# A gated delta-rule layer on one core: strict triangles built from PSUM, correction matrices kept in three buffers, and a new order of VectorE's work in each pass

## What is computed

```python
q, k, v = silu(causal_conv4(x @ w_qkv))             # 4 taps in time, per channel
g, beta = -exp(A_log) * softplus(a + dt_bias), sigmoid(b)
q, k = l2norm(q) * DK ** -0.5, l2norm(k)
def step(state, inp):
    state = state * exp(g_t)
    delta = (v_t - einsum('kv,k->v', state, k_t)) * b_t
    state = state + einsum('k,v->kv', k_t, delta)
    return state, einsum('kv,k->v', state, q_t)
y = rms_norm(out * silu(z)) @ w_out
```

## Time and profile before

| | before |
|---|---|
| median of 3 runs | 3218.49 us (3217.93 to 3222.51) |
| the profiled execution's own time | 3209.48 us |
| its span, first to last instruction | 3207.7 us |
| TensorE busy | 2926.0 us, 91% |
| VectorE busy | 2951.7 us, 92% |
| GpSimd busy | 2218.9 us, 69% |
| ScalarE busy | 1798.5 us, 56% |
| mean granted TensorE clock | 0.975 of full speed |
| chain that ended last, by engine | VectorE 62%, TensorE 22%, ScalarE 8%, issue 5% |

### The profile page before, as it was taken

How to read it: one execution, slowest core, us unless ns; L and a number is a source line. 1 busy time by engine, 2 the same in 40 slices (tenths; PEclk the granted TensorE clock), 3 DMA queues, 4 the chain that set the end, 5 groups by cost and what they waited for, 6 DMA issues and landing times.

```text
span 3207.7 us, 56507 instructions
## 1 busy us (share of the span) xinstructions
PE 2926.0 (91%) x18444; PEld 2394.4 (75%) x18444; DVE 2951.7 (92%) x9293; ACT 1798.5 (56%) x4175; POOL 2218.9 (69%) x2394
## 2 busy tenths in 40 slices
PE   7942899999999999999999999999999999999997
PEld 4421678787878877878778877788787787877876
DVE  4997899999999999999999999999999999999996
ACT  3321555565556655565555655566555665656554
POOL 0003677877777777777777777787777777777764
PEclk9975999999999999999999999999999999999999
DMA  2002555555555555555555555555555565555653
GB/s 64 1 1 66 151 142 144 143 149 156 140 146 138 156 151 140 143 141 156 144 146 135 151 157 142 144 138 155 151 145 139 142 159 146 149 134 146 159 143 85
DMA packets 541829, 427.99 MB, mean 133 GB/s; under 512 B 247009, under 2 KB 450785, under 8 KB 541537
## 3 DMA queue, kind: packets, MB, share of 16 engines
q1 hardware_dynamic: 476000, 222.98, 25.6%
q0 software_dynamic: 65536, 201.39, 24.0%
HBM read 345.61 MB, written 45.09 MB: 122 GB/s over the span
## 4 chain that ended last, share of the span: by engine, by line
DVE 62%; PE 22%; ACT 8%; issue 5%; DMA 1%; POOL 1%; POOLq 1%; DVEq 0%; SPq 0%; ACTq 0%
DVE mix L1222 12%; DVE qkv L1181 9%; PE ps L584 4%; DVE E L1169 4%; DVE rows L1201 4%; PE ps L522 3%; DVE xg L1148 3%; PE ps L526 3%; PE ps L556 3%; PE ps L569 3%; PE ps L576 3%; DVE xr L1238 3%; ACT L824 2%; ACT L841 2%; DVE outer L1234 2%
## 5 line engine op out<-in xcount | busy, mean ns | idle before, releaser
L958 POOL DMA_INDIRECT rows<-table,idx_all x1024 | 1200.1, 1172 | 382.7 <-issue 280.3
L813 ACT ACTIVATE qkv<-qkv 128x512 f32<-128x512 f32 x256 | 161.4, 630 | 603.8 <-DVE qkv L1181 603.8
L942 POOL TENSOR_SCALAR xg<-xg,rms 128x128 f32<-128x128 f32 x520 | 407.3, 798 | 7.0
L576 PE MATMUL ps<-XT,E 128*128 128x128 f32 x3072 | 400.5, 277 | 0.0
L556 PEld LDWEIGHTS ps<-X,AT 128*128 128x128 f32 x3072 | 363.4, 192 | 35.7 <-DMA X<-whole 17.9
L1222 DVE SCALAR_TENSOR_TENSOR mix<-rows,zc,mix 128x256 f32<-128x256 f32 x896 | 381.3, 491 | 0.4 <-ACT zc L824 0.4
L556 PE MATMUL ps<-X,AT 128*128 128x128 f32 x3072 | 375.2, 275 | 3.3 <-DMA X<-whole 3.3
L576 PEld LDWEIGHTS ps<-XT,E 128*128 128x128 f32 x3072 | 368.7, 192 | 0.0
L946 POOL COPY gn<-gates 128x8 f32<-128x8 f32 x64 | 12.3, 193 | 481.3 <-SPq L330 262.2
L950 POOL TENSOR_SCALAR gm<-cst,gn 128x128 f32<-128x128 f32 x512 | 340.3, 680 | 6.5
L808 ACT ACTIVATE raw<-ps 128x512 f32<-128x512 f32 x256 | 152.9, 597 | 313.5 <-PE ps L522 313.5
(11 more groups left out here) (165 smaller groups left out, 6172.5 us busy)
## 6 DMA issues: line engine op xcount, KB each, us to landing
Wvz<-wvz SPq DMA_DIRECT2D x64, 512.0 KB, 3.2
xb<-xnT SPq DMA_DIRECT2D x64, 512.0 KB, 4.5
whole<-AT SPq DMA_DIRECT2D x128, 256.0 KB
X<-whole SPq DMA_DIRECT2D x128, 256.0 KB, 4.2
XT<-whole SPq DMA_DIRECT2D x128, 256.0 KB, 4.7
wo<-woh SPq DMA_DIRECT2D x65, 256.0 KB, 4.4
Wkq<-wkq SPq DMA_DIRECT2D x64, 256.0 KB, 2.9
rows<-table,idx_all POOLq DMA_INDIRECT x1024
```

Of the source, the lines that this page charges most:

```text
L576: done = mm(ps[:, 4 + g, (a % 4) * P:(a % 4 + 1) * P], E[:, a, :], src[:, a, :], start=True, stop=True)
L942: pool.tensor_scalar(xg[:, a, :], xg[:, a, :], rms[:, a:a + 1], None, ALU.mult).then_inc(sm["y_p"], 1)
L958: pool.indirect_dma_start(rows[:, m, :], None, table[:, :], bass.IndirectOffsetOnAxis(ap=idx_all[:, f // 4, c:c + 1], axis=0)).then_inc(ga ...
```

## The change

- `triangle` multiplies straight out of PSUM bank 6, by the negated scales `nscol` (new), eight instructions that each count up `at_v`. The masked copy `km` and the added identity are gone: elements outside the strict triangle and the sign are dealt with further on (the elimination adds instead of subtracting; the off-diagonal blocks are taken as they are).
- `E` becomes three buffers `Es`, one per level, which GpSimd fills with identities once, ahead of the first step. At level 0 VectorE writes only the off-diagonal blocks (`copy_predicated`), at level 1 ScalarE copies them (`second_level`, four copies of 32 partitions), at level 2 VectorE copies one 64x64 block per task. The level matrices leave the constants.
- Since bank 6 is held until the triangles are read, `projection(1)` goes to bank 7 and `squares(0)` to bank 3.
- On VectorE the three taps of k stand inside the first half of the expert sums, after four of its eight instructions, and `half_v` comes behind the other four. The corrections of `RV` stand ahead of the taps of v. `scaled_y(0)` stands ahead of the elimination.
- The copy `xb` of the normalized input, and its transfer of 512 KB per step, are gone: `projection(4)` and `(5)` read `xnT`. `Y` now lies in `X`.

`output_weights`, which computes MT on VectorE, is the same before and after.

```diff
-C_ID, C_LE, C_GT, C_SU, C_EYE, C_MS = 0, 1, 2, 3, 4, 6
-NC = C_MS + len(LEVELS)
+C_ID, C_LE, C_GT, C_EYE, C_OFF = 0, 1, 2, 3, 5
+NC = 6
...
+    off = (p // (2 * BL) == j // (2 * BL)) & (p // BL == j // BL + 1)
...
-        E = sb("E", [P, TASKS, P])
-        Y = E
+        Es = [sb(f"E{lv}", [P, TASKS, P]) for lv in range(len(LEVELS))]
+        Y = X
...
-                sp.dma_start(xb[:, :, :], xnT[:, :, bass.ds((f // HEADS) * N, N)]).then_inc(sm["xb_in"], 16)
...
-                    sp.wait_ge(sm["at_v"], at("at_v", g + 1))
+                    sp.wait_ge(sm["at_v"], at("at_v", 4 * g + 4))
...
-                    bank = (7, 6, 7, 6, 7, 6)[u]
+                    bank = (7, 7, 7, 6, 7, 6)[u]
...
-                    pe.wait_ge(sm["e_v"], at("e_v", 2 * lv + g + 1))
+                    if lv == 1:
+                        pe.wait_ge(sm["e_s"], at("e_s", 2 * g + 2))
+                    else:
+                        pe.wait_ge(sm["e_v"], at("e_v", lv + g + 1))
...
                     products(0, 6)
-                    pe.wait_ge(sm["tap_s"], at("tap_s", 2))
-                    squares(0, 7)
-                    pe.wait_ge(sm["km_v"], at("km_v", 1))
+                    if back:
+                        pe.wait_ge(sm["x_s"], at("x_s", 2))
+                    squares(0, 3)
                     projection(1)
+                if front:
+                    pe.wait_ge(sm["ssk_v"], at("ssk_v", 1))
...
-                    pe.wait_ge(sm["ssk_v"], at("ssk_v", 1))
+                    pe.wait_ge(sm["tap_s"], at("tap_s", 4))
                     products(1, 7)
-                    pe.wait_ge(sm["tap_s"], at("tap_s", 4))
+                    pe.wait_ge(sm["at_v"], at("at_v", 8))
                     squares(1, 6)
...
+                def second_level(g):
+                    act.wait_ge(sm["e_t"], at("e_t", 3 + g))
+                    for p0, c0 in ((32, 0), (96, 64)):
+                        A(Es[1][p0:p0 + 32, 4 * g:4 * g + 4, c0:c0 + 32],
+                          ps[p0:p0 + 32, g, :].rearrange("p (a i) -> p a i", a=4)[:, :, c0:c0 + 32], ACT.Copy).then_inc(sm["e_s"], 1)
...
                     take_XT(0, 1)
+                    second_level(0)
+                    second_level(1)
...
+            for buf in Es:
+                pool.tensor_copy(buf[:, :, :], mask(C_ID, TASKS)).then_inc(zeroed, 1)
...
                     dve.wait_ge(sm["e_t"], at("e_t", 2 * lv + g + 1))
-                    V.tensor_tensor(E[:, 4 * g:4 * g + 4, :], ps[:, g, :].rearrange("p (a i) -> p a i", a=4), mask(C_MS + lv, 4), ALU.mult)\
-                        .then_inc(sm["e_v"], 1)
+                    e, new = Es[lv][:, 4 * g:4 * g + 4, :], ps[:, g, :].rearrange("p (a i) -> p a i", a=4)
+                    if lv == 0:
+                        done = V.copy_predicated(e, mask(C_OFF, 4).bitcast(U32), new)
+                    else:
+                        done = V.tensor_copy(e[64:128, :, 0:64], new[64:128, :, 0:64])
+                    done.then_inc(sm["e_v"], 1)
...
                     for a in range(4 * g, 4 * g + 4):
-                        st.did(V.scalar_tensor_tensor(out=AT[:, a, :], in0=km[:, a // R, :], scalar=scol[:, a:a + 1], in1=DT[:, a, :],
-                                                      op0=ALU.mult, op1=ALU.mult))
-                    st.wait()
-                    V.tensor_tensor(AT[:, 4 * g:4 * g + 4, :], AT[:, 4 * g:4 * g + 4, :], mask(C_ID, 4), ALU.add).then_inc(sm["at_v"], 1)
+                        V.scalar_tensor_tensor(out=AT[:, a, :], in0=ps[:, 6, (a // R) * P:(a // R + 1) * P], scalar=nscol[:, a:a + 1], in1=DT[:, a, :],
+                                               op0=ALU.mult, op1=ALU.mult).then_inc(sm["at_v"], 1)
...
-                    V.tensor_tensor(km[:, :, :], ps[:, 6, :].rearrange("p (t i) -> p t i", t=4), mask(C_SU, 4), ALU.mult).then_inc(sm["km_v"], 1)
...
-                    expert_mix(0)
+                    expert_mix(0, 2)
+                if front:
+                    for d in (1, 2, 3):
+                        tap(0, d)
+                if back:
+                    expert_mix(2, 4)
                     st.wait()
                     dve.sem_inc(sm["half_v"], 1)
-                if front:
-                    for d in (1, 2, 3):
-                        tap(0, d)
-                if back:
                     second_gated(nx)
-                    level(1, 0)
-                    level(1, 1)
...
+                if back:
+                    scaled_y(0, 1, "y0_t", "ys0_v")
...
-                    eliminate(0, 4)
-                if back:
-                    scaled_y(0, 1, "y0_t", "ys0_v")
-                if front:
-                    eliminate(4, HB - 1)
+                    eliminate(0, HB - 1)
```

More of the change, by code:

```diff
@@ L66, in constants @@
     p, j = i[:, None], i[None, :]
-    def level(n):
-        off = (p // (2 * n) == j // (2 * n)) & (p // n == j // n + 1)
-        return np.eye(P) - off
+    off = (p // (2 * BL) == j // (2 * BL)) & (p // BL == j // BL + 1)
     eye = np.broadcast_to(np.eye(BL).reshape(1, BL * BL), (P, BL * BL))
-    m = [np.eye(P), p <= j, p > j, p < j, eye[:, :P], eye[:, P:]] + [level(n) for n in LEVELS]
+    m = [np.eye(P), p <= j, p > j, eye[:, :P], eye[:, P:], off]
     m = np.stack([np.asarray(a, np.float32) for a in m], 1).reshape(P, NC * P)
@@ L525, in projection @@
                             for k in range(KD):
-                                done = mm(ps[:, bank, (t % 2) * 256:(t % 2) * 256 + 256], xb[:, k, t * P:(t + 1) * P],
+                                done = mm(ps[:, bank, (t % 2) * 256:(t % 2) * 256 + 256], xnT[:, k, pn * N + t * P:pn * N + (t + 1) * P],
                                           Wvz[:, k, 2 * P:4 * P], start=k == 0, stop=k == KD - 1)
@@ L805, in take @@
                         act.wait_ge(sm["conv_v"], last("conv_v", u + 3))
-                    bank = (7, 6, 7, 6)[u]
+                    bank = (7, 7, 7, 6)[u]
                     w = cwkq[:, u, 3:4] if u < 2 else cwv[:, u - 2, 3:4]
@@ L1205, in expert_dots, with expert_mix @@
                                     half_of(prob_all[:, n // 4, (n % 4) * 16:(n % 4) * 16 + 16], hf), ALU.mult).then_inc(sm["dot_v"], 1)
-                def expert_mix(hf):
-                    dve.wait_ge(sm["silu_e"], at("silu_e", hf + 1))
-                    for k in range(hf * (K // 2), (hf + 1) * (K // 2)):
+                def expert_mix(k0, k1):
+                    dve.wait_ge(sm["silu_e"], at("silu_e", k0 // 4 + 1))
+                    for k in range(k0, k1):
                         for s in range(2):
@@ L1237, in eliminate @@
                         v = x[:, :, j + 1:HB, 0:m]
-                        last_row[0] = st.did(V.tensor_tensor(v, v, o, ALU.subtract))
+                        last_row[0] = st.did(V.tensor_tensor(v, v, o, ALU.add))
                 def lower_products():
@@ L1319, in one_pass @@
                     level(0, 1)
-                    expert_mix(0)
-                    st.wait()
-                    dve.sem_inc(sm["half_v"], 1)
+                    expert_mix(0, 2)
                 if front:
@@ L1326, in one_pass @@
                 if back:
+                    expert_mix(2, 4)
+                    st.wait()
+                    dve.sem_inc(sm["half_v"], 1)
                     second_gated(nx)
-                    level(1, 0)
-                    level(1, 1)
                     if place["u"]:
```

38 lines of the change are left out of this document (18 added, 20 removed).

## The result

The changed kernel is slower: 3293.15 us in the median of 4 runs (3284.49 to 3296.89) against 3218.21 us (4 runs, 3212.65 to 3222.51) of the kernel before, ratio 1.023, 95% interval 1.0204 to 1.0256. The profiled execution took 3296.89 us.

The account below looks back on a forecast made before the run. It took a loop through GpSimd's gathers and scales as the bound, with VectorE's load equally long. Terms of +0.8 us a step gave +50 us, other effects −2, so 3218.5 + 48 = 3266 us, range 3200 to 3310.

Parts of the forecast that it names:

- What bounds the kernel: One step: a loop through GpSimd's gathers and scales to TensorE's transposes and tail closes it; VectorE's load closes another, equally long.
- GpSimd's loop: Differences, experts' first half, `half_v`, eight gathers, square root, eight scales, transposes, TensorE's tail, next differences: 44.53 us a step.
- VectorE's load: Masks, `km` and identity adds go: about 3.8 us of 44.53 leave VectorE; level 0's `copy_predicated` taken as 0.67 us.
- the rival of twice a mask: Level 0's `copy_predicated` costs double a mask, delaying mix, k's taps and `half_v`: +43 us more, 3309 us; chance 10%.
- Release: `half_v`, which lets GpSimd's gathers start, comes at D+11.35 instead of D+8.42 behind k's taps: +2.9 us a step.
- Gathers: GpSimd's eight gathers are held less by VectorE's two-SBUF-input instructions: −1.0 us a step, bounds 0 and −1.9.
- Scales: GpSimd's eight scales: VectorE's second mix still falls onto them, MT no longer: −0.3 us a step, bounds 0 and −1.5.
- Tail: From GpSimd's last scale to the next differences: 15.1 us instead of 15.87, VectorE now waiting for `ks_t`: −0.8 us.
- The sum: Per step, +2.9 − 1.0 − 0.3 − 0.8 = +0.8 us; over sixty-two steps +50 us.
- GpSimd is freed enough: First gather to last scale falls by more than 2.1 us, so the kernel gets faster: 3132 us, halfway 3175; 17%.
- The gathers don't matter: GpSimd's timing is a coincidence; TensorE alone is left with its holes filled: −2.7 a step, 3050 us; 5%.
- ScalarE is not late: z is emptied in time for the second difference matmul, so the step grows only +0.2: 3230 us; chance 10%.

Follow-up runs that it names:

- the first four experiments: Changed kernel with k's taps behind the release, 0.9906; corrections behind v's taps, 0.994; both orders undone, 0.9985; eight unused matmuls in TensorE's wait, 1.0073; against the kernel before.

## Why the prediction was right

The forecast was 3266 us, the result 3293, inside the range of 3200 to 3310 and on the forecast side. By its steps:

- *What bounds the kernel.* Right: GpSimd's loop became the bound, TensorE stood before the transposes (2.1 us a step in the timeline, 161 us of waiting in all, against "some 2 us, over 100").
- *VectorE's load.* 2.9 us a step left it, not 3.8. What was removed came to about 3.8; other instructions grew, such as the first two outer products of the elimination, which now stand beside GpSimd's scales and took 0.29 and 0.35 us in the step from 1541.71 on, where they had taken 0.16 and 0.17. This didn't matter, as assumed. `copy_predicated`, the copies of level 1 on ScalarE and those of level 2, groups of instructions (xcount | busy us, mean ns | idle before):

```profile
L1179 DVE COPY_PREDICATED E<-cst,ps 128x512 f32<-128x512 uint32 x128 | 93.7, 733 | 14.4 <-PE ps L550 13.3
...
L823 ACT ACTIVATE E<-ps 32x128 f32<-32x128 f32 x256 | 69.0, 269 | 6.8 <-PE ps L550 0.6
L1181 DVE COPY E<-ps 64x256 f32<-64x256 f32 x128 | 54.7, 428 | 91.0 <-PE ps L550 91.0
```

  0.73 us where I took 0.67, so the rival of twice a mask falls; 0.43 for a 64x256 copy, against 0.33 taken.
- *Release.* +2.73 against +2.9. The second difference matmul does wait for ScalarE's z, and `level_E(0)` begins at D+2.20 instead of D+1.72: 0.48 late, taken as 0.6. Its row before, where D was 1500.34:

```profile
1502.06 1.97 PE L556 MATMUL ps<-X,AT 128*128 128x128 f32 x16
```

- *Gathers* with the square root. −1.44 against −1.0: more of the held gathers were freed than I assumed, within the bounds.
- *Scales.* +0.12 against −0.3, at the wrong side of nothing: eight take 6.49 us against 6.37. The reading that failed is "MT no longer does": VectorE's MT still falls onto the scales. Two of the eight scales taken singly, the first beside MT and the second beside the mix, and VectorE's MT, which ends at 1521.18 and is followed by the mix:

```profile
1520.14 1.43 POOL L948 TENSOR_SCALAR xg<-xg,rms 128x128 f32<-128x128 f32 x1
1521.57 0.84 POOL L948 TENSOR_SCALAR xg<-xg,rms 128x128 f32<-128x128 f32 x1
...
1519.89 1.29 DVE L1308 TENSOR_TENSOR MT<-kq,DT 128x512 f32<-128x512 f32 x2
```

  The three after the mix take 0.60 each. By the Trainium skill's rule (SBUF — State Buffer, section Who interferes with whom) a scale beside the mix would have taken 1.0 us, an estimate; at 0.84 the trace again shows part of the overlap that the rule denies. Beside MT, whose instructions take 0.69 each, the same rule gives an estimate of 0.69 + 0.60 = 1.29 us, and the trace's 1.43 shows none of that overlap.

- *Tail.* −0.79 against −0.8, with VectorE's new wait for `ks_t`, 1.27 us.
- The sum is +0.62 a step against +0.8.
- *Missing term.* The granted clock. I gave TensorE's new wait of 2 us the price of its own length. It brought the lower clock to 22 steps more, 37 us, as much as the longer step itself (37). The sum had 50 for the latter, so the miss of 27 us between 3266 and 3293 is 37 less 13, and a few us elsewhere. That the two errors have opposite signs is luck.
- *The rivals.* "GpSimd is freed enough" needed the stretch from first gather to last scale 2.1 us shorter; it is 1.3. It counted the level copies among what was freed, but the level masks had read one of their two inputs from PSUM before as well (`E<-ps,cst`); only the triangles and the identity adds had two in SBUF. "The gathers don't matter" falls with the wait at L490. "ScalarE is not late" was near in size only: it is late by 0.48.

The mechanism was right, a part of the size for a reason not seen. What the prediction did not see either: the new kernel's penalty depends on the chip (1.023 and 1.0405 for the same code), and on chip C the wait that the prediction names is not there. Its mechanism holds for the trace of the result and, by the first four experiments, for chip A.

## What to carry to other kernels

Where two loops of nearly the same length close a step, a reordering that serves one is to be costed in the other: here, on the new masks and on chip A, each order alone gained 0.3 to 0.5 us a step and both together lost as much, and taking 2.9 us from VectorE gained nothing because its chain began with something late. Before work is moved ahead of a release, the slack of the engine that waits for the release is to be read; here it had none. A wait of TensorE in a kernel that otherwise keeps it busy can cost more than its length; count the steps of uneven length, and fill the wait with harmless matmuls to see what of the loss is the clock.

## What the runs showed of the hardware

- The granted clock fell behind a wait of 1.91 us in 30 of 62 steps, in 10 with the same wait and a step one microsecond shorter (chip A), and with the wait filled in none (one step began with it). What decides which steps are hit was not tried.
- A GpSimd scale of 128x128 took 0.60 us at the least, 0.84 beside VectorE's mix (128x256, two inputs in SBUF) and 1.43 beside MT (128x512, two inputs in SBUF).
- A step of the same kernel was 1.4 us longer on another chip (46.56 against 45.15), where results of TensorE were taken by ScalarE 2.7 and 4.6 us after the matmuls' end in the stretch with the gathers. A ranking within 1% from one chip need not hold on another.
